# The expert block stage of a Mamba-and-experts layer: the first products of a block ahead of the turn of the next one

## The reference

```
h   = layernorm(x)
probs = softmax(h @ Wg);  top_vals, top_idx = top_k(probs, 2);  top_vals /= sum(top_vals)
y_e = relu(h @ W1[e] + b1[e]) @ W2[e] + b2[e]         # W1[e] 128x256, W2[e] 256x128
out = x + layernorm(sum over the two experts of share * y_e)
```

## Time and profile before

| | |
|---|---|
| median of 3 runs | 1099.35 us (1098.7 to 1101.97) |
| the profiled execution | 1096.12 us |
| its span | 1093.6 us |
| busy: PE, DVE, ACT, POOL | 802.2, 727.3, 655.6, 678.7 us |
| block stage, first normalised rows to last return issued | 769.8 to 1017 us |
| final stage | from there to 1093.6 us |

### The profile page before, as it was taken

How to read it: one execution, slowest core, us unless ns; L and a number is a source line. 1 busy time by engine, 2 the same in 40 slices (tenths; PEclk the granted TensorE clock), 3 DMA queues, 4 the chain that set the end, 5 groups by cost and what they waited for, 6 DMA issues and landing times.

```text
span 1093.6 us, 24134 instructions
## 1 busy us (share of the span) xinstructions
PE 802.2 (73%) x7431; PEld 651.8 (60%) x7431; DVE 727.3 (67%) x2183; ACT 655.6 (60%) x1449; POOL 678.7 (62%) x1019
## 2 busy tenths in 40 slices
PE   4799999889898898898898987420676766667000
PEld 2587787667677676677677776420566655556000
DVE  6578888887977987888878875461344443444475
ACT  4687878667676776676676674110455654554375
POOL 7156655767767867767677666764255555556444
PEclk9899999999999999999999998655789899998555
DMA  6000000000000000000000004002222232222475
GB/s 188 3 4 2 5 5 3 15 16 12 19 14 17 17 17 16 15 18 17 14 17 13 18 13 119 31 32 64 74 77 76 74 81 74 80 74 65 115 199 147
DMA packets 60014, 50.83 MB, mean 46 GB/s; under 512 B 10438, under 2 KB 53729, under 8 KB 59888
## 3 DMA queue, kind: packets, MB, share of 16 engines
q1 hardware_dynamic: 51248, 32.23, 11.2%
q0 software_dynamic: 8640, 17.06, 4.9%
HBM read 25.76 MB, written 23.37 MB: 45 GB/s over the span
## 4 chain that ended last, share of the span: by engine, by line
PE 35%; POOL 17%; issue 15%; ACT 11%; DVE 9%; DMA 6%; another core or an unknown queue 4%; DVEq 2%; SPq 1%; ACTq 0%; POOLq 0%
POOL expert_rows L1277 5%; PE bank L851 4%; PE bank L648 3%; DMA moe_pair<-expert_results 3%; PE bank L923 3%; POOL y L1010 3%; PE bank L1879 3%; PE bank L650 2%; PE bank L649 2%; POOL zt L1003 2%; PE bank L906 2%; PE bank L835 2%; PE bank L638 2%; PE bank L837 2%
## 5 line engine op out<-in xcount | busy, mean ns | idle before, releaser
L1904 POOL DMA_INDIRECT expert_results<-moe_y,moe_dest x142 | 140.2, 987 | 123.3 <-DVE moe_y L1897 81.5
L1277 POOL DMA_INDIRECT expert_rows<-xall,row_index x128 | 133.6, 1044 | 44.4 <-issue 39.8
L648 PE MATMUL bank<-thi,whi 128*128 128x512 f32 x224 | 107.5, 480 | 38.7 <-ACT xtok L943 32.6
L935 ACT ACTIVATE m<-bank 128x512 f32<-128x512 f32 x128 | 70.2, 593 | 89.9 <-PE bank L837 89.4
L1817 PE MATMUL bank<-ident,moe_h 128*128 128x128 f32 x142 | 31.5, 307 | 89.5 <-ACT moe_h L1805 85.9
L1019 DVE TENSOR_TENSOR mg<-bank,m 128x512 f32<-128x512 f32 x128 | 82.3, 685 | 17.2 <-PE bank L851 16.0
L1010 POOL TENSOR_TENSOR y<-y,zt 128x256 f32<-128x256 f32 x64 | 56.3, 879 | 58.4 <-issue 34.0
L1879 PE MATMUL bank<-moe_w,moe_hid 128*128 x568 | 88.1, 303 | 4.0 <-ACT moe_hid L1865 2.6
L650 PE MATMUL bank<-thi,wlo 128*128 128x512 f32 x224 | 90.9, 406 | 0.0
L649 PE MATMUL bank<-tlo,whi 128*128 128x512 f32 x224 | 90.6, 405 | 0.0
L1824 ACT ACTIVATE moe_t_hi<-bank 128x256 fp32r<-128x256 f32 x71 | 27.2, 383 | 94.8 <-remote 85.4
(11 more groups left out here) (231 smaller groups left out, 2567.6 us busy)
## 6 DMA issues: line engine op xcount, KB each, us to landing
moe_block_in<-expert_rows SPq DMA_DIRECT2D x71, 132.0 KB
moe_pair<-expert_results SPq DMA_DIRECT2D x16, 512.0 KB, 4.2
out_dram<-moe_outb SPq DMA_DIRECT2D x16, 256.0 KB, 2.5
expert_results<-moe_y,moe_dest POOLq DMA_INDIRECT x142
parts<-csplit SPq DMA_DIRECT2D x128, 4.0 KB
rows<-csplit SPq DMA_DIRECT2D x128, 4.0 KB
expert_rows<-xall,row_index POOLq DMA_INDIRECT x128
expert_rows<-spare_row SPq DMA_DIRECT2D x9, 132.0 KB, 2.1
```

What stands on the lines that cost most here:

```text
L648: PE.matmul(bank[:], whi[:, w], thi[:], start=True, stop=False)
L935: SE.activation(m[:, hf * HH:(hf + 1) * HH, :], banks[2 + hf][:].rearrange("p (h l) -> p h l", l=P), ACT.Exp).then_inc(m_ready.sem, 1)
L1277: PL.indirect_dma_start(buckets, bass.IndirectOffsetOnAxis(row_index[:, k, t:t + 1], 0), xall[:, t, :], None).then_inc(scattered, 16)
L1904: PL.indirect_dma_start(back_d, bass.IndirectOffsetOnAxis(dest[:, b % BACK, n:n + 1], 0), yout[:, b % BACK, n, :], None, bounds_check=2 * ...
```

## The change

In PE's program of the block stage, `pe_up(b)` is issued ahead of `pe_turn(b + 1)`. The first turn, of block 0, stays ahead of the loop, and `pe_down(b - 1)` stays last. Nothing else differs; the waits inside the steps are the same.

```diff
         pe_count(pe)
         pe_turn(pe, 0)
         for b in range(NBLK):
+            pe_up(pe, b)
             if b + 1 < NBLK:
                 pe_turn(pe, b + 1)
-            pe_up(pe, b)
             if b:
                 pe_down(pe, b - 1)
         pe_down(pe, NBLK - 1)
```

## The result

The changed kernel takes 1106.36 us (median of 14 runs, 1102.1 to 1111.04). Beside them the kernel before took 1100.66 us (14 runs, 1097.72 to 1103.37). The ratio is 1.0053, with a 95% interval of 1.0033 to 1.0073: slower by 5.7 us. The forecast was +2.2 us, and rival B was +15 to +16.

A forecast was written before the change was run, and what follows sets the result against it. The order of waits, with PE's completions reaching waiters late, was taken to pace the block stage, no engine being full. Terms 0 + 0 + 1.5 + 0.7 = +2.2 us on the median 1099.35 gave 1101.5 us, range 1085 to 1115.

The forecast's parts named there:

- rival B: Block stage: second products miss the moment of mid-run, so the long round becomes the rule; 1115 us, chance 0.24.
- item 2: PE's block loop: the turn of b+1 starts later where it used a gap, yet the round keeps its length; 0 us.
- Step 1: PE's block loop: products of b start up to 0.37 us sooner where the turn waited, in some half the rounds; 0 us.
- Step 2: PE's block loop: turn 1.3 us later, second products 0.2 to 0.3 us later, all before the release; 0 us.
- Step 3: Block stage: turns let out ahead of the other held completions, in six rounds, are lost; +1.5 us, bound 0 to 6.
- Step 4: Start of the block stage: the turn of block 1 follows block 0's products, POOL's first return comes later; +0.7 us.
- The release: Sign, block stage: copies that wait start, as before, 1.9 us behind POOL's fourth issue of a run.
- Rival A: Block stage: both kinds of round become the short one, 15 rounds losing 1.0 us each; 1084 us, chance 0.29.
- Rival C: Whole kernel: the reordering changes nothing, as PE waits for the same inputs; 1099.4 us, chance 0.05.
- Rival D: PE in the block stage: it really works until the release, so its own time bounds; 1109 us, chance 0.04.
- ACT's 84 us: Sign at ACT's copy act_hi (L1824): 84.3 us of waits labelled remote; their moving to PE would count against the forecast.

The follow-up runs named there:

- before with 0.2 us more: Kernel before plus two unused transposes (the spare transposes) on PE ahead of the second products, turn unmoved; ratios 0.9972, 0.9989, 1.0015 on three chips.
- two products less: Both orders with the two lo-by-hi products (L1855) left out of the six first products; 1071.77 us (0.9994) old order, 1072.16 us (0.9996) new.
- turn last: Changed kernel with the turn of b+1 also behind the second products, pe_down(b-1); 1092.16 us (1.0168) on the third chip, 1087.04 us on the fourth.

## Where the prediction was right, and where it fell short

The forecast was slower by 2.2 us, and the measurement says slower by 5.7. The sign is right and the time lies inside the stated 1085 to 1115. But that range was made wide enough for two rivals of opposite sign, so its holding says little, and the sum behind the forecast is short of most of the effect. The term that failed is the 0 us of item 2. I sorted the parts by two lengths: from the first normalised rows to POOL's first return (start-up), and from POOL's first to its last return (stage), in us, one profiled execution each.

| kernel, chip | start-up | stage |
|---|---|---|
| before, first | 9.89 | 236.61 |
| after, first | 10.58 | 248.27 |
| before, second | 8.79 | 237.05 |
| after, second | 10.77 | 242.67 |
| before with 0.2 us more, third, fourth, fifth | 10.11, 10.22, 10.15 | 222.57, 220.86, 221.82 |
| after, fifth | 10.76 | 223.31 |
| before / after, two products less, fourth | 8.85 / 10.00 | 219.44 / 221.95 |
| turn last, third, fourth | 11.85, 11.83 | 241.12, 239.54 |

*Step 1, the products earlier: right.* The first matmul of the products stands at 852.93, 0.05 us behind the low part's end at 852.46 + 0.42 = 852.88. It was worth nothing.

*Step 2, the turn later: its times right, its price not.* The turn ends 1.66 us after POOL's first issue (1.6 to 1.7 said; up to 2.5 us in rounds at the lower clock level), with the copy 0.04 us behind. The cover was to be 0.36 us, the low part starting in any case later than the copy's end. It shrank to 854.59 - 854.55 = 0.04 us, as DVE now reaches the low part earlier. It still held: the next products start 855.06 - 852.47 = 2.59 us after POOL's first issue, before 888.88 - 885.91 = 2.97. What failed is the sentence "so the round keeps its length". I checked that everything ends before the release. I put at nothing that the second products, which end 0.1 us later against POOL's issues, mostly no longer come out in mid-run. The reading behind it was wrong too: the prediction takes DVE's result at 890.96 for a completion that came late, and its round has no term for the landing of a return. DVE stood at the destination rows until 890.13 for that landing. Without that term the sum could not show what a short round loses when its products are held to the release, about 0.9 us. The text names this, in rival B, with its point of decision: "It decides as soon as the block's last products, 0.3 us later through the turn ahead of them, miss the moment of mid-run". I held it for less likely than the forecast. In the first chip's pair of traces the rounds came out as B says, 29 long ones for 15; that the 0.1 us is the reason is not shown.

*Step 3, turns let out early: they are lost, the price not told apart.* It was given +1.5 us, up to 6. Of the six rounds in which the second turn's copy came at 4.2 to 5.1 us after POOL's first issue, after on the first chip has none: there it starts at 5.9 us or later. Where nearly all rounds are long the loss sits inside rival B's.

*Step 4, start-up: right in size, in part by luck.* POOL's first return came at 780.62, 0.97 us later, but the first normalised rows were later as well, and the start-up itself grew by 0.69 us; 0.7 was taken. The item's own parts, 1.3 - 0.66 us less the turn's wait, give 0.64 at most, and before alone reads 9.89 in one trace and 8.79 in another. Start-up is longer in every pair of the table, by 0.69, 1.98 and 1.15 us, and also on the chips that hold nothing, so it does not need a held completion. The spare transposes with the turn in its old place read 10.1 to 10.2 us, so how much of it is the turn's place is not shown. The two rows of after, ACT's first normalising of the stage and POOL's first return:

```profile
770.04 0.88 ACT L1805 ACTIVATE moe_h<-moe_block_in 128x128 f32<-128x128 f32 x2 [25.82 <-DMA moe_block_in<-expert_rows]
...
780.62 1.08 POOL L1904 DMA_INDIRECT expert_results<-moe_y,moe_dest  x1 [26.53 <-DVE moe_y L1897]
```

*The release: right.* 858.41 - 856.33 = 2.08 us behind the fourth issue, 1.9 said.

*Rival A fell:* 3 short rounds are left, not 31. *Rival C fell* on the three chips on which after ran: each ratio is above 1 with its interval. *Rival D fell in its price:* on the last three chips the same instructions have their copies promptly, and neither 0.22 us less nor 0.2 us more of PE's work lengthened or clearly shortened the time there. Whether the late part on the chips that hold is PE's writing of the results or the signal behind it, no run tells. My list took it for a sign against the forecast if ACT's 84 us moved to PE. They did not: ACT's wait at the copy grew, and PE's 64.1 us at L1854 stand against 47.5 us that it waited at the turn before.

*Rival B was right in kind and too large.* It came to +15 us by 16 short rounds of 1.0 us. The profiled pair on the first chip gives 248.27 - 236.61 = +11.7 us in the stage, the pair on the second chip +5.6. The medians differ by 5.7 us on the first chip, and on the second by a ratio that makes 7.9 us of 1092.67. With some 1 us of start-up in it, B's mechanism is worth at most about 5 to 7 us there in the mean of executions. Where nothing is held, after costs +2.3 us, and the interval of that ratio reaches from 0.6 to 5.5 us. That this is the sum of the forecast is luck: 1.5 us of that sum are turns let out early, which need a hold. What part of the 5 to 7 us is this cost without a hold is open.

*What stays open.* What holds PE's completions on two chips and not on three was not found, nor whether it is the chip itself. That POOL's returns do it rests on when the waits end, 1.9 to 2.1 us behind the fourth issue; the kernels without them ran where nothing was held. That the second products miss a moment by 0.1 us rests on sorting the rounds of the first chip's two traces, and those of the second fit it only in part. The kernel that shifts only them ran three times and never on a chip that holds. That the turn's place does it, and not the time of the second products, is the rival that is left.

No version that does the same work is faster than the kernel before by more than 0.3%.

## What to carry to other kernels

When a wait ends late for a reason that the profile can't name, don't only ask whether the moved work ends before the release. Ask whether some rounds escape the hold, which piece of work does, and how near to the edge it stands: the escapes were worth 1 us each here, and a shift of 0.1 us in the order of PE's work went with losing most of them on one chip. Before a late instruction is put down to one cause, read what its engine did just ahead of it: DVE's result was late for a landing that the instruction in front waited for, and that landing is the pace of the stage where nothing is held. When a change makes one wait grow, add up all waits of that engine: twice here (11 us in the main pair, 25 us without POOL's returns) the wait had moved. And run both kernels on a second chip before the size of such an effect is believed.

## What the runs showed of the hardware

The same program, the kernel before, took 1100.66 and 1092.67 us on the two chips that hold completions and 1071.57, 1071.1 and 1071.48 on the three that don't: 2.8% between the ends, five times the effect under study. Most of the difference sits in the block stage (236.6 and 237.1 us on the first two; 219.4 to 222.6 on the others for kernels with its order, before itself having no trace there), and it does not follow the granted clock from 782 to 1005 us: 0.95 and 0.86 in the two slow stages, 0.94 in the spare transposes' on the fifth chip.

On two of the chips completions of PE reached ACT and DVE about 3 us behind the modelled end while POOL issued a run of indirect DMAs, most of them together about 1.9 to 2.1 us after the last issue. On the third the copy started 0.04 us behind the turn's modelled end (853.09 + 0.38 to 853.51) with the same DMAs under way. The Trainium skill, Perfetto Trace Analysis, "Tensor Engine Instruction (MATMUL, LD_WEIGHTS)", has the semaphore pushed when PSUM acknowledges the write and propagated after that; it gives no time for either. Counted from the modelled end, these traces show a few hundredths of a microsecond in one case and 3 us in the other, behind the same instruction; which of the two steps takes them, they don't show.

An indirect DMA costs POOL 0.98 us, issued every 1.29 us, in the traces of every chip. The destination rows that wait for a return to land start 2.6 to 2.9 us behind its issue (853.76 to 856.33 in after and 887.19 to 890.13 in before on the first chip, 852.92 to 855.72 in after on the fifth). Replacing the 142 of them by plain DMAs of SP gave 32 us, and DVE's waits for the landings went from 49.7 to 0.4 us; POOL was busy only 62% of the span.
